# Perceiver layer on one core: the self-attention pipeline with its output projection of the cross attention one step ahead of the normalisation

## The reference

```python
x = x + xattn(ctx_1024, layernorm(x), mask, ...)   # 16 heads of 64; keys: 1601 context rows and the 64 latents
x = x + attn(layernorm(x), W_q, b_q, ...)          # causal self-attention over 64 latents, 16 heads of 16, with rope
x = x + ffn(layernorm(x), w1, b1, w2, b2, wr, br)  # 4 experts of 1024 hidden, the best 2 weighted by softmax
```

## Time and profile before

| what | us |
|---|---|
| median of 3 runs | 2098.61 |
| span of the profiled execution | 2101.0 |
| block 2, first ScalarE instruction to last VectorE instruction | 1697.27 to 1879.41 |
| TensorE busy in the whole span | 1954.0 (93%) |
| one step of block 2 in its middle (c1 to c1) | 1767.36 to 1784.83 |

### The profile page before, as it was taken

One profiled execution on the slowest core, in us unless ns is written; L12 is line 12 of the kernel. 1 busy time (PEld: TensorE's weight loads), 2 busy tenths in 40 slices (PEclk: granted clock), 3 DMA queues, 4 the chain that ended last, 5 costly groups with the idle time before them and its releaser, 6 DMA issues. The chain is left out here.

```text
span 2101.0 us, 34809 instructions
## 1 busy us (share of the span) xinstructions
PE 1954.0 (93%) x11540; PEld 1745.0 (83%) x11540; DVE 1400.3 (67%) x3072; ACT 958.6 (46%) x1616; POOL 596.5 (28%) x652
## 2 busy tenths in 40 slices
PE   5899999999999999999999999999999968769998
PEld 5789898989898988888888888898988857648887
DVE  6676667767676767776767676767666437745555
ACT  4354545454545454454545453545454322225443
POOL 4050404141323223131415050504040047621110
PEclk9899999999999999999999999999999978869999
DMA  6101010101010101010000000000100130011100
GB/s 214 59 4 36 15 46 7 44 15 34 15 34 15 34 15 34 15 34 25 24 25 24 25 24 25 24 25 24 37 15 1 41 111 31 1 50 41 41 20 21
DMA packets 40874, 69.52 MB, mean 33 GB/s; under 512 B 4721, under 2 KB 26609, under 8 KB 40817
## 3 DMA queue, kind: packets, MB, share of 16 engines
q1 hardware_dynamic: 40816, 68.77, 10.8%
HBM read 58.27 MB, written 10.49 MB: 33 GB/s over the span
## 5 line engine op out<-in xcount | busy, mean ns | idle before, releaser
L218 PE MATMUL o_bank<-probT,val 128*128 128x512 f32 x2496 | 685.2, 410 | 7.6 <-DVE probT L786 5.0
L218 PE MATMUL s_bank<-keyT,qkT 128*128 128x416 f32 x3072 | 633.1, 355 | 0.0
L218 PEld LDWEIGHTS s_bank<-keyT,qkT 128*128 128x128 f32 x3072 | 570.5, 188 | 20.8
L218 PEld LDWEIGHTS o_bank<-probT,val 128*128 128x128 f32 x2496 | 438.6, 189 | 90.3 <-DVE probT L786 11.6
L745 ACT ACTIVATE prob<-prob,negmax 128x1665 f32<-128x1665 f32 x128 | 216.1, 1688 | 381.5 <-DVE negmax L813 381.5
L786 DVE TENSOR_TENSOR probT<-t_bank,probT 128x512 fp32r<-128x512 f32 x416 | 284.9, 688 | 151.8 <-ACT probT L725 144.5
L808 DVE CUSTOM_DVE_ANT_0 prob<-s_bank,bias 128x416 f32<-128x416 f32 x512 | 297.0, 587 | 102.2 <-PE s_bank L218 99.4
L725 ACT ACTIVATE probT<-t_bank 128x512 fp32r<-128x512 f32 x416 | 243.3, 592 | 250.0 <-PE t_bank L878 248.0
L878 PE MATMUL t_bank<-ident,prob 128*128 128x128 f32 x1664 | 253.3, 275 | 8.4 <-DVE probT L786 6.0
L878 PEld LDWEIGHTS t_bank<-ident,prob 128*128 128x128 f32 x1664 | 200.3, 141 | 46.5 <-DVE probT L786 13.4
L343 POOL TENSOR_TENSOR small<-stats 128x9 f32<-128x9 f32 (+1 forms) x32 | 7.0, 217 | 766.1 <-DVE stats L297 766.1
(11 more groups left out here) (196 smaller groups left out, 2139.6 us busy)
## 6 DMA issues: line engine op xcount, KB each, us to landing
stage<-in_ctx SPq DMA_DIRECT2D x48, 512.0 KB, 3.7
q_scratch<-qstage SPq DMA_DIRECT2D x4, 1024.0 KB, 4.5
y_scratch<-ystage SPq DMA_DIRECT2D x32, 128.0 KB, 1.7
yraw<-y_scratch SPq DMA_DIRECT2D x8, 512.0 KB, 3.8
stage<-in_w SPq DMA_DIRECT2D x4, 1024.0 KB, 5.4
w2raw<-in_w SPq DMA_DIRECT2D x4, 1024.0 KB, 5.6
q<-q_scratch SPq DMA_DIRECT2D x15, 256.0 KB, 2.7
mask<-in_mask SPq DMA_DIRECT2D x16, 200.1 KB, 3.2
```

Source lines behind the costliest of these rows:

```text
L218: mm = pe.matmul(out, weights(a), moving(b), start=first and n == 0, stop=last and n == 2)
```

## The change

The lag of a1 becomes -1. In step s all engines now run a1 for tile s + 1 and a2n and a2 for tile s. Nothing else is different: the written order of the parts, the instructions of each part, their semaphores and their buffers stay. a1 now runs in steps -1 to 6 instead of 0 to 7.

```diff
         for s in range(-2, RT + 4):
-            for name, lag in (("d3n", 4), ("a1", 0), ("d3", 4), ("c1", 2), ("d1", 3), ("b1", 1), ("c1m", 2),
+            for name, lag in (("d3n", 4), ("a1", -1), ("d3", 4), ("c1", 2), ("d1", 3), ("b1", 1), ("c1m", 2),
                               ("a2n", 0), ("b1v", 1), ("a2", 0), ("d2", 3), ("c2", 2), ("b2", 1), ("c3", 2), ("a0", -2)):
```

## The result

The changed kernel takes 2134.33 us, the median of 4 runs (2132.45 to 2137.31), against 2100.64 us (2097.41 to 2104.21, 4 runs) before. The ratio is 1.0163 with a 95% interval of 1.0147 to 1.0179: slower, by 33.7 us.

What follows compares the result with a forecast made beforehand. A chain over four engines, not TensorE, was taken to bound block 2's steps. Start +15.2, then steps +3.2, +5.6, +5.4, +5.4, -0.8 gave +34.0 us: span 2135.0, median 2133, range 2123 to 2147.

Steps and rivals of the forecast that it cites:

- The mechanism: In block 2, a1 must wait for `y_low`, GpSimd's last work of a step: 4.2 us later in a middle step.
- The predicted sign in the profile: TensorE idles before nearly each a1 from tile 2 on, about 4 us in a middle step, released by GpSimd's `ysplit`.
- The start: From block 2's start to the first c1: b1 of tile 0 8.5 us late, the first c1 15.2 us late.
- The steps: Five steps from c1 to c1 after the first c1: +3.2, +5.6, +5.4, +5.4 and -0.8 us.
- the 22 to 23 given as a sign: Length in us that a middle step, c1 to c1, would show in the changed kernel's trace.
- Two terms inside: Price of a1, taken as 4.31 us, and time from c1 to the end of `y_low`, 17.4 then 18.4 us.
- The free gain of nothing: TensorE's 3.10 us idle before a2 stays, since VectorE's order and not `rstd` holds the normalisation; gain 0.
- The clock rival: TensorE sinks to the lower clock for whole steps, a1 5.23 and c1 3.68 us: +48 us, 2147; chance 12%.

Runs made afterwards that it cites:

- e1: Changed kernel with a0 one step further ahead too (lag -3); 2103.49 us, ratio 1.0022 to the kernel before.
- e2: Changed kernel with GpSimd's `y_low` ahead of its key blocks instead of behind them; 2123.56 us, ratio 1.0120 to the kernel before.
- e3: Kernel before with a0 of tiles 2 to 7 one step later (lag -1), a1 not moved; 2134.21 us, ratio 1.0163.
- e4: Changed kernel with 24 extra matmuls keeping TensorE busy ahead of the wait for `y_low`, tiles 2 to 7; 2129.85 us, ratio 1.0149 to the kernel before.
- e5: e1 with the normalisation a2n moved from behind c1m to right behind a1; 2106.39 us, ratio 1.0030 to the kernel before.
- e6: Kernel before with only the normalisation a2n moved ahead of c1m in the written order; 2103.03 us, ratio 1.0020.
- e8: e5 with 16 extra matmuls keeping TensorE busy ahead of the score transposes' wait for the exponential; 2093.09 us, ratio 0.9971 to the kernel before.
- e11: e8 with a1 of tiles 1 and 2 placed behind a2 of their steps; 2093.27 us, ratio 0.9967 to the kernel before.
- e10: e6 with 16 extra matmuls keeping TensorE busy ahead of the wait for the exponential; 2086.03 us, ratio 0.9938 to the kernel before.
- e9: Kernel before with 24 extra matmuls ahead of a2's wait for the normalisation, tiles 2 to 7; 2090.02 us, ratio 0.9959.

## Why the prediction was right

It said 2133 us, with 2123 to 2147; 2134.33 came. The span was said as 2135.0 and is 2135.4; it stands 1.1 us above the median, where 2.4 was taken. Its steps, with the times of the profiled executions:

- *The mechanism* (a1 held by `y_low`, the last of GpSimd's step) is shown by e1, e2 and e3. e1 and e3 move a0, ScalarE's rounding included, against a1; e2 moves GpSimd's `y_low` alone. The predicted sign in the profile, GpSimd as named releaser, appeared only in e4; in the changed kernel the profile says "issue".
- *The start*: b1 8.5 us late was predicted, and it is 8.6 (29.4 us into the block against 20.8); the first c1 15.2, measured 15.7 (49.8 against 34.1).
- *The steps*: +3.2, +5.6, +5.4, +5.4 and -0.8 predicted; +2.4, +6.2, +6.0, +6.0 and -1.2 measured. The two after that, predicted as unchanged, are +1.2 and -1.0. In all 34.0 against 35.3. The middle steps, 23.5 us, are just over the 22 to 23 given as a sign.
- *Two terms inside were off and partly cancelled.* a1 took 4.47 to 5.46 us, 5.0 in the mean of the six, where 4.31 was taken: 4 us more over the six; a1 of tile 1 took 4.60 where 5.23 was taken. The time from c1 to the end of `y_low` was 16.5, 18.2, 17.8 and 17.7 us where 17.4 and three times 18.4 were taken: 2.4 us less in the sum. So it is in part luck that the total came so close. The lower clock, which had fallen on the work behind a2, now falls on a1: the output projection behind a2 takes 0.95 to 1.19 us in the middle steps of the changed kernel, and took 1.40 to 1.63 before.
- *The free gain of nothing* held: the wait before a2 stayed at 3.11 us. e5 and e6 show that VectorE's order can take it away, that a wait of 2.0 to 2.3 us for the exponential then stands before the score transposes, and that this alone gains nothing.
- *The clock rival* (+48) did not come: c1 takes 1.94 us in all steps that have an a1, so the clock is back within one a1. The granted clock is 0.50 at the beginning of each of the six. This agrees with the loop of the Trainium skill (TensorE: Matmul & The Clock Gate, HAM oscillation), which waits in each round and starts its matmuls on the lower clock. Behind the 3.1 us before a2 the clock falls only after the work has started (1.00 from 1794 to 1798, 0.63 from 1798 to 1802). What it costs in this kernel, as an estimate from the rows: the six a1 took 30.0 us, against 20.9 before, so about 9 us of the 35.3. e4 got 4.4 us back, with 3.6 us lost again by extra matmuls that ran past the wait.

What stays open: the medians of e8 to e11 gained 2.6 to 5.4 us less on the kernel before than their blocks did (e10: 13.8 against 18.6). A start that varies by some 3 us can be part of it. Outside the block single profiled executions range from 1912.5 us (e1) to 1921.2 (e11) with the same instructions there, and no run here says whether that is chance. Nor was it tried how few extra matmuls would do.

## What to carry to other kernels

When a stage of a software pipeline is moved a step ahead, look for the producer that stays behind: its distance shrinks by one step, and what matters then is where in its engine's step the producer is issued, not how busy that engine is (GpSimd was busy for 28% of the span). A stage is worth moving only if its result is late; here it had been 4.8 us early already. And in a pipeline of engines that wait for each other, ask which matmuls run behind TensorE's idle stretch: moving a wait can cost more by the clock than it gains.

## What the runs showed of the hardware that was not expected

- Work that computes nothing made the kernel faster: 24 extra matmuls (3.04 us) in an idle stretch of 3.1 us took 1.2 to 1.4 us off each middle step of the kernel before, and 0.41% off the whole (e9).
- The lower clock can come late: in e5 TensorE stood idle until 1778.2, the granted clock was still 1.00 from 1778 to 1780 and fell near 1780, so the price was paid by c3 and a1, not by what followed the wait. In the kernel before it fell as the wait ended (0.96 in 1774 to 1776, 0.50 in 1776 to 1778, the wait to 1775.6).
- GpSimd and VectorE slow each other down. The same normalisation took 0.41 us alone and 1.35 to 1.53 us beside a GpSimd tensor-tensor, and then it ended 0.15 us after that had ended, wherever it had started: 1775.53 after 1775.38 before (L1210), 1797.80 after 1797.65 in the changed kernel (L1210), 1768.64 after 1768.49 in e8 (`y_low`). So 1.35 us is no size of its own: it is the rest of GpSimd's instruction. GpSimd's key blocks took 3.00 us beside VectorE's, and 2.09 in e10, where VectorE's had ended and the third layer norm ran for 1.13 us beside them.
